# A windowed-attention and convolution kernel: tap products on POOL in row 4, packed transposes, outputs gathered in one evacuation, projection in four matmuls

## What is computed

```python
x = x + window_attention(gn(x))   # 7x7 windows, shifted by 3; 8 heads of 8 channels; q,k,v and output projections
x = x + binary_conv3x3(gn(x))     # signs of input and kernel, scaled by box means of |input| and means of |kernel|
x = x + ternary_conv3x3(gn(x))    # signs of the kernel, input in fp32
x = x + gated_conv1d(gn(x))       # project in, 4 causal taps along the tokens, silu, gate, project out
```

```python
attn = softmax(q * scale @ k.T + relative_position_bias + shift_mask)   # 49 x 49 for each head
out  = (attn @ v).reshape(49, 64) @ proj_weight.T + proj_bias
```

## Time and profile before

| | |
|---|---|
| median of 3 runs | 211.79 us (211.61 to 211.81) |
| profiled execution: span | 207.2 us, 4.6 less than that median; the page gives no other time of its own |
| PE busy | 195.3 us, 94% |
| PE weight loads | 135.0 us, 65% |
| DVE busy | 160.1 us, 77% |
| ACT busy | 141.2 us, 68% |
| POOL busy | 105.9 us, 51% |
| TensorE clock granted | full in every slice of the page |

### The profile page before, as it was taken

One profiled execution on the slowest core, in us unless ns is written; L12 is line 12 of the kernel. 1 busy time (PEld: TensorE's weight loads), 2 busy tenths in 40 slices (PEclk: granted clock), 3 DMA queues, 4 the chain that ended last, 5 costly groups with the idle time before them and its releaser, 6 DMA issues.

```text
span 207.2 us, 6854 instructions
## 1 busy us (share of the span) xinstructions
PE 195.3 (94%) x2751; PEld 135.0 (65%) x2751; DVE 160.1 (77%) x323; ACT 141.2 (68%) x299; POOL 105.9 (51%) x117
## 2 busy tenths in 40 slices
PE   7978999999999999699999999999989999999994
PEld 2446887888878878478878788555446655543331
DVE  3575789987887879997876977299998768869463
ACT  2348598688778887668887965807585547789751
POOL 0359999813322369622369301775954521548470
PEclk9999999999999999999999999999999999999999
DMA  6980000000000000000000000000124450110513
GB/s 199 440 332 3 3 3 3 3 3 3 5 3 0 3 5 3 0 3 3 5 0 3 3 5 0 3 0 3 45 68 94 116 130 5 37 39 14 180 39 116
DMA packets 5021, 9.97 MB, mean 48 GB/s; under 512 B 768, under 2 KB 3840, under 8 KB 4864
## 3 DMA queue, kind: packets, MB, share of 16 engines
q1 hardware_dynamic: 4848, 9.21, 14.0%
q10 hardware_dynamic: 144, 0.34, 0.4%
HBM read 5.03 MB, written 1.61 MB: 32 GB/s over the span
## 4 chain that ended last, share of the span: by engine, by line
PE 71%; DVE 12%; ACT 5%; issue 5%; POOL 2%; DMA 2%; ACTq 0%; DVEq 0%; POOLq 0%
PE turned L827 11%; PE outs L847 10%; PE scores L816 9%; PE scores L946 6%; PE qkv L787 4%; PE qkv L797 4%; PE turned L1028 3%; PE scores L1002 3%; PE scores L962 3%; PE qkv L1016 3%; PE scores L1003 3%; DVE mx L1173 2%; DMA xw<-xw_in 2%; PE outs L869 2%; DVE d L1178 2%
## 5 line engine op out<-in xcount | busy, mean ns | idle before, releaser
L1173 DVE TENSOR_REDUCE mx<-scores 113x16 f32<-113x784 f32 x32 | 30.9, 965 | 7.5 <-PE scores L816 7.2
L827 PE MATMUL turned<-cst,d 113*113 113x113 f32 x256 | 33.3, 273 | 2.8 <-DVE d L1178 2.7
L212 POOL TENSOR_TENSOR kex<-ks,cst 128x784 f32<-128x784 f32 (+1 forms) x16 | 23.6, 1474 | 22.9 <-ACT ks L510 22.7
L827 PEld LDWEIGHTS turned<-cst,d 113*113 113x113 f32 x256 | 27.8, 178 | 10.5 <-issue 6.5
L531 ACT ACTIVATE pt<-turned 113x392 f32<-113x392 f32 x64 | 28.4, 496 | 6.9 <-PE turned L827 5.8
L1178 DVE TENSOR_TENSOR d<-scores,mx 113x784 f32<-113x784 f32 x32 | 31.2, 976 | 1.1
L501 ACT ACTIVATE scores<-rel 113x784 f32<-113x784 f32 x32 | 26.3, 820 | 7.5 <-PE scores L757 3.9
L847 PEld LDWEIGHTS outs<-vsb,pt 113*49 113x49 f32 x1024 | 26.1, 125 | 6.7 <-issue 2.9
L847 PE MATMUL outs<-vsb,pt 113*49 113x18 f32 x1024 | 29.2, 199 | 0.3 <-DVE x L1203 0.3
L816 PE MATMUL scores<-kex,qs 32*49 32x196 f32 x512 | 28.2, 332 | 0.0
L338 POOL TENSOR_TENSOR rstd<-ve,mhalf 128x1 f32<-128x1 f32 (+1 forms) x15 | 8.7, 579 | 32.8 <-DVE ve L1139 32.6
(11 more groups left out here) (123 smaller groups left out, 373.8 us busy)
## 6 DMA issues: line engine op xcount, KB each, us to landing
p<-parts SPq DMA_DIRECT2D x14, 112.5 KB, 2.2
x<-x_in SPq DMA_DIRECT2D x1, 1568.0 KB, 9.9
out<-xw SPq DMA_DIRECT2D x8, 196.0 KB, 1.9
xs<-xs SPq DMA_DIRECT2D x8, 98.5 KB, 2.1
xw<-xw_in SPq DMA_DIRECT2D x2, 392.0 KB, 4.9
xw<-xw_in SPq DMA_DIRECT2D x1, 784.0 KB, 6.7
ker<-ker_in SPq DMA_DIRECT2D x2, 288.0 KB, 10.2
p3x<-parts SPq DMA_DIRECT2D x8, 60.0 KB, 2.0
```

The source lines that it names most:

```text
L212: return engine.tensor_tensor(kex[:, par, :, a * WT:b * WT], ks[:, a * WT:b * WT].rearrange("p (o t) -> p o t", o=1).broadcast_to([P, 4, n ...
L827: mm = pe.transpose(ps_t[j][0:WK, n * P:n * P + WK], d[0:WK, k % 2, h:h + 2, :].rearrange("p a b -> p (a b)")[:, 0:WK], ident[0:WK, 0:WK])
L1173: dve.tensor_reduce(top, sc, AXX, ALU.max).then_inc(max_done, 1)
```

## The change

Five edits:

- `tap_weights` goes from DVE (behind its half 2R+1 of R = 8) to POOL, behind the key mask of R = 4. Its five instructions signal one by one, so PE waits for five.
- The constant with which the transposes are made was the identity; it is now a permutation, `packed`, that puts both runs of 49 next to each other and the padding last. The transposes lie 98 columns apart and each writes over the padding of the one before. exp reads 392 elements in one run.
- `gather` packs in the same way, and ACT evacuates its two outputs in one instruction, 128x196. The window's parity stays in the partition half, the image in the columns.
- `project` therefore takes four matmuls: for each parity b and image w, the half b of the diagonal weights (128x64) on 98 columns, to the partition half w of ps_x, with a strided output in 14 runs of seven.
- Of the twelve fillers eight stay; behind them come 16 fp32 matmuls of zeros, 32 rows by 49 columns of weights, 196 columns each, over four row positions and two column positions, which add to the score banks.

```diff
--- before.py
+++ after.py
@@ -35,7 +35,7 @@
 SCALE = HD ** -0.5
 
 
-CI = dict(ident=(0, P), avg=(P, P), diff=(2 * P, P), ones=(3 * P, P), kmask=(4 * P, 4), apart=(4 * P + 4, 3 * WT))
+CI = dict(packed=(0, P), avg=(P, P), diff=(2 * P, P), ones=(3 * P, P), kmask=(4 * P, 4), apart=(4 * P + 4, 3 * WT))
 NCI = 4 * P + 4 + 3 * WT
 
 WI, WIDTHS = {}, []
@@ -89,7 +89,7 @@
         vsb = sb("vsb", [P, 2, NW * 4 * 2, 18])
         rc = sb("rc", [P, NW, NH])
         osb = sb("osb", [P, NW, C])
-        att = sb("att", [P, WS, NW, WS])
+        att = sb("att", [P, 2 * WS, 2, WS])
         bqs = sb("bqs", [P, 1])
         bt = sb("bt", [P, 1])
 
@@ -401,6 +401,14 @@
                 pool.tensor_tensor(w2[:], above[:], w2[:], ALU.subtract).then_inc(w2_ready, 1)
                 pool.wait_ge(w2_ready, 2)
 
+            def tap_weights():
+
+                pool.wait_ge(ld_late, 16)
+                for n in range(4):
+                    pool.tensor_tensor(g12[:, n // 2, n % 2], ww("wx"), ww("cw")[:, n * P:(n + 1) * P], ALU.mult)\
+                        .then_inc(g12_ready, 1)
+                pool.tensor_scalar(wo4[:], ww("wo"), 4.0, None, ALU.mult).then_inc(g12_ready, 1)
+
             def border(t, value):
 
                 pool.memset(t[..., ::PAD - 1, :], value)
@@ -439,6 +447,8 @@
                     binary_signs()
                 if R == 2:
                     ternary_signs()
+                if R == 4:
+                    tap_weights()
                 if g > 0 and r == 3:
                     row_sums(g)
                 if g > 1 and r == 0:
@@ -529,7 +539,7 @@
                 if k >= 2:
                     act.wait_ge(pv_done, k - 1)
                 act.activation(pt[0:WK, k % 2, j].rearrange("p n (w t) -> p n w t", w=2),
-                               ps_t[j][0:WK, :].rearrange("p (n w t) -> p n w t", n=4, w=2)[:, :, :, 0:WT],
+                               ps_t[j][0:WK, 0:4 * WQ].rearrange("p (n w t) -> p n w t", n=4, w=2),
                                ACT.Exp).then_inc(exp_done, 1)
 
             def evac_att(R):
@@ -537,15 +547,8 @@
                 act.wait_ge(ot_done, R + 1)
                 if R > 0:
                     act.wait_ge(proj_done, R)
-                for w in range(2):
-                    for b in range(2):
-
-                        last = act.activation(
-                            att[64 * w:64 * w + 64, :, b:NW:2].rearrange("p i m j -> p m i j"),
-                            ps_qk[64 * b:64 * b + 64, 0:2 * P].rearrange("p (m t) -> p m t", t=P)
-                            [:, :, 64 * w:64 * w + WT].rearrange("p m (i j) -> p m i j", j=WS),
-                            ACT.Identity)
-                last.then_inc(att_ready, 1)
+                act.activation(att[:], ps_qk[:, 0:2 * WQ].rearrange("p (m a j) -> p a m j", m=2, j=WS),
+                               ACT.Identity).then_inc(att_ready, 1)
 
             def absolutes(g):
 
@@ -739,7 +742,7 @@
 
         @block.tensor
         def _(pe):
-            ident = cc("ident")
+            packed = cc("packed")[0:WK, 0:WK]
 
             def mix(j, n, count, ps):
 
@@ -759,7 +762,14 @@
 
             pe.wait_ge(idle_set, 1)
             for b in range(4):
-                mm = filler(bk[b], 3)
+                filler(bk[b], 2)
+            zero = idle[:].bitcast(F32)
+            for _ in range(2):
+                for b in range(4):
+                    for w in range(2):
+                        mm = pe.matmul(bk[b][64 * w:64 * w + WT, 0:4 * WT], zero[32 * b:32 * b + 32, 0:WT],
+                                       zero[32 * b:32 * b + 32, 0:4 * WT], start=False, stop=True,
+                                       skip_group_check=True)
             mm.then_inc(bits_set, 1)
             pe.wait_ge(ld_c, 16)
             mix(0, 1, 1, ps_t[0])
@@ -824,9 +834,8 @@
                     pe.wait_ge(exp_done, 2 * k - 1 + j)
                 for n in range(4):
                     h = 8 * j + 2 * n
-                    mm = pe.transpose(ps_t[j][0:WK, n * P:n * P + WK],
-                                      d[0:WK, k % 2, h:h + 2, :].rearrange("p a b -> p (a b)")[:, 0:WK],
-                                      ident[0:WK, 0:WK])
+                    mm = pe.transpose(ps_t[j][0:WK, n * WQ:n * WQ + WK],
+                                      d[0:WK, k % 2, h:h + 2, :].rearrange("p a b -> p (a b)")[:, 0:WK], packed)
                 mm.then_inc(t_done, 1)
 
             def values(k):
@@ -857,8 +866,8 @@
                     pe.wait_ge(att_ready, R)
 
                 for m in range(NW // 2):
-                    mm = pe.transpose(ps_qk[:, m * P:m * P + WK],
-                                      osb[0:WK, 2 * m:2 * m + 2].rearrange("p a c -> p (a c)"), ident[0:WK, 0:WK])
+                    mm = pe.transpose(ps_qk[:, m * WQ:m * WQ + WK],
+                                      osb[0:WK, 2 * m:2 * m + 2].rearrange("p a c -> p (a c)"), packed)
                 mm.then_inc(ot_done, 1)
 
             def project(R):
@@ -866,8 +875,12 @@
                 pe.wait_ge(o_ready, min(R + 1 + (R == NR - 2), NR))
                 if R > 0:
                     pe.wait_ge(res_done, R)
-                pe.matmul(ps_x, ww("wp"), att[:].rearrange("p i a j -> p (i a j)"),
-                          start=True, stop=True).then_inc(proj_done, 1)
+                for b in range(2):
+                    for w in range(2):
+                        y = ps_x[64 * w:64 * w + 64].rearrange("p (i m b j) -> p i m b j", i=WS, m=2, b=2)
+                        mm = pe.matmul(y[:, :, :, b, :], ww("wp")[:, b * C:(b + 1) * C],
+                                       att[:, w * WS:(w + 1) * WS], start=True, stop=True)
+                mm.then_inc(proj_done, 1)
 
             def copied_by(R):
 
@@ -1032,7 +1045,7 @@
             pe.wait_ge(w1_ready, 2)
             pe.wait_ge(w2_ready, 2)
             pe.wait_ge(ld_late, 16)
-            pe.wait_ge(g12_ready, 1)
+            pe.wait_ge(g12_ready, 5)
             channel_sums(0, 0)
             values(NP - 1)
             channel_sums(0, 1)
@@ -1235,13 +1248,6 @@
                                              4.0 / (NTAP * C) / (NTAP * C), None, ALU.mult)
                 last.then_inc(aw_ready, 1)
 
-            def tap_weights():
-
-                for n in range(4):
-                    last = dve.tensor_tensor(g12[:, n // 2, n % 2], ww("wx"), ww("cw")[:, n * P:(n + 1) * P], ALU.mult)
-                last = dve.tensor_scalar(wo4[:], ww("wo"), 4.0, None, ALU.mult)
-                last.then_inc(g12_ready, 1)
-
             def signs(g):
 
                 dve.tensor_scalar(sg1[:, g, 1:1 + HW, 1:1 + HW], x[:, g], sg[:, col(1, g), 0:1], 0.5,
@@ -1272,9 +1278,6 @@
                     variances(2, 2, 3, mixed)
                 if R == 3:
                     channel_scales()
-                if R == 8:
-                    dve.wait_ge(ld_late, 16)
-                    tap_weights()
                 if g > 0 and r == 1:
 
                     dve.wait_ge(res_done, R - 1)
@@ -1417,7 +1420,8 @@
 
     c = np.zeros((P, NCI), np.float32)
     i = np.arange(P)
-    c[i, CI["ident"][0] + i] = 1
+    order = np.concatenate([np.arange(WT), 64 + np.arange(WT), np.arange(WT, 64)])
+    c[order, CI["packed"][0] + np.arange(WK)] = 1
     for o, s in ((0, 0.5), (1, 0.5)):
         c[i, CI["avg"][0] + (i ^ o)] = 0.5
     c[i, CI["diff"][0] + i] = 0.5
```

## The result

| | before | changed |
|---|---|---|
| median of 4 runs | 211.70 us (211.55 to 211.81) | 206.47 us (205.47 to 208.75) |
| the four runs of the change, time / span | | 208.75 / 206.9, 205.6 / 203.8, 207.35 / 205.6, 205.47 / 203.7 |
| profiled execution, span | 207.2 us | 206.9 us (the run of 208.75) |
| ratio | | 0.9745, 95% interval 0.9693 to 0.9798 |

The ratio leaves out the run of 208.75 us, which is over 1.5% above the fastest of its kernel. The change is faster by 2.5%, 5.2 us by the medians, where 3.1 were forecast (3.2 from 211.79) and 207.9 was the lower end of the range. Two things are odd at once. The profiled spans differ by only 0.3 us. And the four runs of the change lie 3 us apart, while each has 1.75 to 1.85 us outside its span; I had counted with 4.6.

A forecast was written before the change was run, and what follows sets the result against it. PE, busy for 94% of the span, was taken as the bound. Terms -2.34 - 1.06 + 0.1 + 0.1 = -3.2 us gave a span of 204.0 and, with 4.6 outside it, 208.6 us; range 207.9 to 210.1.

The forecast's parts named there:

- What lies around the span: Whole run: the median time was 4.6 us above the profiled span of 207.2, and this was taken to stay.
- The tap products, -2.34: Row 9: taking five instructions off DVE makes it as short as row 5, -2.34 us (bounds 1.78 to 2.34).
- Evacuation and projection, -1.06 + 0.2: Attention: one evacuation removes ACT's waits in rows 7 and 11, -1.06; projection in four adds 0.1 inside, 0.1 at its end.
- Packed transposes, 0: Attention: packed transposes and exp reading 392 elements in one run bring no gain and no loss, 0.
- The start, 0: Start: the small matmuls end at 6.2, before the moments' matmul at 6.61, so 0; +1.0 if only four tiles run at once.
- Rival 1: Start becomes late: small tiles take eight rounds, +1.0, or the clock is still low for the nine fillers, +2.6; 12%.
- rose only between 6.5 and 7.3: Start: PE's clock rose only then, behind twelve full matmuls without a gap; given as evidence for a late start.
- Rival 2: Projection in each row: its four matmuls do not overlap, or runs of seven halve their pace; 213.5 us, 8%.
- Rivals 3 and 4: Attention: 3, moved work hidden less well, half the gain lost, 210.2, 10%; 4, PE waits for what is late next, 211.8, 2%.

The follow-up runs named there:

- e1: The changed kernel again, no edit: 205.65 to 207.24 us in six executions.
- e2: The changed kernel with the start of before (twelve full fillers, no small matmuls): 205.60 us median.
- e3: The kernel before with only the new start (eight fillers and 16 small matmuls): 210.68 us median, ratio 0.9991.
- e4: The kernel before with only the tap products moved to POOL in row 4: 206.51 us median.
- e6: The kernel before with the tap products still on DVE, but in row 4 instead of row 8: 206.50 us median.
- e5: The changed kernel with the full start and the tap products back on DVE in row 8: 210.71 us median.
- e7: The changed kernel with the full start and the gathered outputs evacuated in four pieces of 64x98 again: 206.84 us.
- e8: The changed kernel with the full start, each projection matmul writing its 98 columns densely instead of in 14 runs of seven: 205.66 us.
- e12: The changed kernel with the full start, transposes 128 columns apart again and exp reading four runs of 98: 205.68 us.
- e9: The changed kernel once more, no edit, to count executions: 205.59 to 208.80 us in five executions.
- e11: The changed kernel with all twelve full fillers and the 16 small matmuls behind them: 205.90 us.

## Why the prediction was wrong

The mechanism in the attention was right, and so was its sum: without a late start the profiled spans are 203.9 (e1) and 203.8 (e2), where 204.0 was forecast. The step that failed is "the median of the runs, 211.79, is 4.6 more, and I take that to stay": what lies outside the span is 1.8 us. That the profiled execution of the change took 208.75, almost the forecast 208.6, is luck: its late start, 3 us, stood in for the 2.8 that were wrong.

- **What lies around the span.** I took a difference between a profiled execution and the median of others for a constant of the chip. It is 1.8 us, for both kernels and in each experiment but e3, where single executions reach 2.5. The rest, 2.8 us, fits time inside the spans of other executions: in 33 of 45 executions of before the mean clock is lower and the time 1.35 us longer or twice that. The profiled execution, at clock 1.000, was one of the other 12's kind. For the first session itself this is inferred from its times. What I had to doubt was there in numbers: a span is taken on one execution, and 4.6 us had no work behind it.
- **The tap products, -2.34.** Measured on the first level: 208.9 to 206.51 (e4), -2.4. But the stall that the edit removes had a second price that no row of the profiled execution shows: the clock behind it. In medians the edit was worth 3.8 (e4 beside 210.32) and e6's 4.9 (206.50 beside 211.43). This is the term that was mis-sized: the fall of the clock stood in it at nothing. e5 and e3 show the place, e4 and e6 that the levels go with the stall.
- **Evacuation and projection, -1.06 + 0.2.** Together -0.91 (e4 to e2), against -0.86. Taken alone the single evacuation is worth 1.24 (e7 against e2, on different chips; 1.18 against e8 on its own). The two rows gave 0.54 each (R=8: 7.49 in e4, 6.95 in e2) for the forecast 0.53, and R=2, which I had not looked at, another 0.15 (7.55 and 7.40). So the projection costs some 0.3, which is what 14 times 0.02 in the row windows make. I had 0.1 for these rows and 0.1 for the end.
- **Packed transposes, 0.** Right: exp takes as long in all three layouts (e12), and the transposes as long as before, 1.05 us for the eight of a half in both.
- **The start, 0.** 0.05 to 0.14 us where the clock rises in time (e9, e1 against e2), 1.5 to 1.9 us in 2 of 15 executions and 3.15 in 2 more. Rival 1 happened, in 4 of 15 executions where I gave it 12%, the profiled one among them, and its price was not 1.0 or 2.6 but 1.5 to 3.15. That the late ones without a trace were late at the start is inferred. Where it has "rose only between 6.5 and 7.3", say more: the moments' matmuls at 6.61 take 0.35 us there and 0.56 at the low level, so the clock had risen by 6.6. Its first mechanism, eight rounds of small tiles, did not come: the tiles ran eight at a time. And the fall behind a wait that e3 shows was in no rival.
- **Rival 2**, the slower one, did not happen: the passes run in pairs, and a dense output changes nothing (e8). **Rivals 3 and 4**: nothing of them; what was "late next" was PE.

On the first level of both, 208.9 goes to 205.6, -3.3 where -3.2 was forecast. The measured -5.2 is this, less 2.8 for the clock behind the stall (in a session in which the times of before all lie on its third level), plus 0.9 for the changed kernel's own late starts.

What stays open: what decides in one execution whether the clock falls behind the stall, and for how long. The same kernel on the same chip shows all three levels. Also open is the one execution of e6 at 208.2, which has neither the stall nor the new start. A candidate that nothing here tests: in e6's profiled execution PE waits 1.15 us for the moments, and behind such a wait of 1.17 the clock fell in e3.

## What to carry to other kernels

Compare the profiled span with spans of the timed executions, or with what lies outside it in another kernel, before you take their difference for a constant: a difference without work behind it is time that the profile did not catch. A stop of TensorE costs more than its length when the clock falls behind it, so a short stall in dense work is worth removing first. At a start, count executions and not one profile: the full zero matmuls were the steadier choice here, and thinning them out saved nothing. When two engines slow each other, moving the work in time can be as good as moving it to another engine (206.50 and 206.51 us here).

## What the runs showed of the hardware

- The granted clock fell behind waits of PE of 1.8 us in one piece, from 1.00 to 0.50, some 0.4 us after the wait's end in e5 and only 2.2 us after it in e3; behind the same wait it did not fall in the profile of before. At a start it fell behind a wait of 1.17 us (e3). It then stayed low through dense work, in e5 at 0.50 in each window from 86 to 92.
- The Trainium skill says that the point at which the clock rises varies from run to run of one kernel (TensorE: Matmul & The Clock Gate, Part 1: The HAM clock gate). The starts of the changed kernel agree: the small matmuls take 1.58 us in one execution, 1.12 in another, and the first projection begins at 11.60 and at 9.21. The three levels of the kernel before say that the fall in mid-kernel varies too.
- Eight tiles of 32 rows by 64 columns ran at once: 32 passes of 196 columns in 0.91 us at the high clock (e11) and 1.58 at the low one, where four tiles bring 16 through in 0.88.
- A DVE product of 128x128 takes 0.28 us beside an idle POOL (e6) and up to 1.93 beside its box sums; on POOL it takes 0.46.
- ACT's time did not depend on whether 392 elements are read from PSUM in one run or in four (e12, 497 ns for both), or in eight (498 in the kernel before), nor PE's on whether it writes PSUM densely or in runs of seven (e8).
